# Finer row steps per expert, and slots of their own for the weights of the last four experts

## The reference

```
logits = x @ gate_w.T                       # 2048 tokens, 64 experts
topk_w, topk_ids = top_k(softmax(logits), 6)
topk_w = topk_w / (sum(topk_w) + EPS)
g, u = split(x @ w_gate_up[e].T)            # 256 -> 2 x 176, for the chosen experts
routed = sum over chosen e of (silu(g) * u * topk_w[e]) @ w_down[e].T
out = routed + shared
```

## Time and profile before

| | us |
|---|---|
| median of the runs (797.34, 799.22, 3540.21) | 799.22 |
| the profiled execution | 796.76 |
| its span | 795.0 |
| start of the expert stage's first transposes on PE | 475.6 |
| end of the last add of the 64 experts | 767.6 |

### The profile page before, as it was taken

One profiled execution on the slowest core, in us unless ns is written; L12 is line 12 of the kernel. 1 busy time (PEld: TensorE's weight loads), 2 busy tenths in 40 slices (PEclk: granted clock), 3 DMA queues, 4 the chain that ended last, 5 costly groups with the idle time before them and its releaser, 6 DMA issues.

```text
span 795.0 us, 12309 instructions
## 1 busy us (share of the span) xinstructions
PE 634.9 (80%) x3072; PEld 481.3 (61%) x3072; DVE 473.9 (60%) x1598; ACT 285.2 (36%) x641; POOL 432.6 (54%) x482
## 2 busy tenths in 40 slices
PE   3688984864998957989888639999999889899930
PEld 2344541532887736767666528888888767677720
DVE  4887785998587777777776333445444434444422
ACT  2146666773244422434334303233323223222200
POOL 2477877220244422566666652576666666577750
PEclk9799998797899977999999769999999999999975
DMA  6347555585288854555563377999999999999667
GB/s 225 123 136 249 202 171 179 180 278 221 75 311 289 318 162 160 188 194 188 193 219 111 101 233 220 248 250 230 241 259 225 231 235 215 215 220 241 98 142 268
DMA packets 86518, 163.88 MB, mean 206 GB/s; under 512 B 11200, under 2 KB 51584, under 8 KB 86464
## 3 DMA queue, kind: packets, MB, share of 16 engines
q1 hardware_dynamic: 64736, 134.26, 51.2%
q0 software_dynamic: 20864, 28.08, 19.2%
q10 hardware_dynamic: 864, 0.93, 0.3%
HBM read 91.51 MB, written 71.71 MB: 205 GB/s over the span
## 4 chain that ended last, share of the span: by engine, by line
PE 34%; DMA 20%; DVE 18%; issue 14%; POOL 8%; another core or an unknown queue 3%; ACT 1%; DVEq 1%; SPq 0%; POOLq 0%; ACTq 0%
DMA acc<-hh,toki 18%; PE psum L839 5%; PE psum L915 5%; PE psum L1072 5%; POOL xs_rows L738 3%; PE psum L994 3%; DVE hh L1620 2%; PE psum L1076 2%; PE psum L1085 2%; POOL acc L778 2%; PE psum L811 2%; PE psum L906 2%; PE psum L821 2%; PE psum L1060 1%
## 5 line engine op out<-in xcount | busy, mean ns | idle before, releaser
L778 POOL DMA_INDIRECT acc<-hh,toki x128 | 188.1, 1469 | 103.8 <-DMA acc<-hh,toki 51.7
L1918 DVE TENSOR_SCALAR hh<-psum,wtok 96x256 f32<-96x256 f32 (+2 forms) x128 | 55.9, 477 | 152.0 <-PE psum L1090 78.9
L738 POOL DMA_INDIRECT xs_rows<-Z,slot x96 | 96.4, 1004 | 58.4 <-DVE slot L1796 32.4
L1072 PE MATMUL psum<-qT,Z 128*128 128x192 f32 (+2 forms) x512 | 106.1, 351 | 0.0
L1072 PEld LDWEIGHTS psum<-qT,Z 128*128 128x128 f32 x512 | 87.6, 192 | 3.0 <-issue 0.4
L656 POOL TENSOR_TENSOR rstd<-mv,neghalf 128x1 f32<-128x1 f32 (+1 forms) x48 | 36.6, 763 | 77.3 <-DVE mv L1408 77.3
L1345 ACT ACTIVATE qT<-psum 128x384 f32<-128x384 f32 (+2 forms) x64 | 33.9, 530 | 113.3 <-PE psum L1060 96.4
L1085 PE MATMUL psum<-Z,hh 128*96 128x256 f32 (+2 forms) x256 | 61.9, 385 | 14.1 <-issue 8.9
L839 PE MATMUL psum<-wt,hTs 128*128 128x512 f32 x128 | 60.6, 617 | 9.4 <-ACT hTs L1169 9.4
L994 PE MATMUL psum<-qT,wt 128*128 128x256 f32 (+1 forms) x192 | 52.6, 431 | 9.7 <-DVE H L1801 8.9
L1085 PEld LDWEIGHTS psum<-Z,hh 128*96 128x96 f32 (+2 forms) x256 | 42.9, 173 | 28.4 <-issue 12.6
(11 more groups left out here) (337 smaller groups left out, 1233.8 us busy)
## 6 DMA issues: line engine op xcount, KB each, us to landing
Z<-in_wexp SPq DMA_DIRECT2D x66, 496.0 KB
xs_rows<-fill SPq DMA_DIRECT2D x64, 272.0 KB, 3.2
kv_rows<-Z SPq DMA_DIRECT2D x12, 688.0 KB, 3.8
Z<-xs_rows SPq DMA_DIRECT2D x32, 204.0 KB
kvb<-kv_rows SPq DMA_DIRECT2D x8, 688.0 KB
Z<-co_rows SPq DMA_DIRECT2D x8, 688.0 KB
Z<-kv_rows SPq DMA_DIRECT2D x8, 688.0 KB
Z<-xs_rows SPq DMA_DIRECT2D x16, 272.0 KB
```

What stands on the lines that cost most here:

```text
L738: pool.indirect_dma_start(out=xs_rows[:, :], out_offset=bass.IndirectOffsetOnAxis(ap=slot[:, t, k:k + 1], axis=0), in_=H[:, t, :], in_offs ...
L778: pool.indirect_dma_start(out=acc[s % 2][:, :], out_offset=bass.IndirectOffsetOnAxis(ap=toki[0:p, g, j:j + 1], axis=0), in_=y_sb[0:p, s, j ...
L1072: m = pe.matmul(pA[par][:, g * CAP:g * CAP + 2 * p], wgu_sb[:, s, k, g * P:(g + 1) * P], xT[:, par, k, 0:2 * p], start=(k == 0), stop=(k = ...
L1918: m = dve.tensor_scalar(y_sb[0:p, s, j, :], pY[par][0:p, j * D:(j + 1) * D], wtok[0:p, g, j:j + 1], None, ALU.mult)
```

## The change

Rows: `PARTS` goes from (128, 128, 112, 112, 96, 96, 96, 96) to (128, 120, 112, 104, 96, 96, 88, 80), so that iterations 1, 3, 6 and 7 have fewer rows, and every iteration from 1 on has a phase of its own. The capacity of each rank is worked out on DVE from six steps of 16 instead of two of 32.

Weights: those of the last four ranks go to four slots of their own, in `X` and in a free part of `hidden`, and are loaded right behind those of ranks 4 to 7, after a wait for `seeded` (all rows of the stream are written) and `ov_ready` 2 (the overflow tables are done). The last refill then leaves out its last four weight loads. PE reads these slots for the last four ranks. The two semaphores of each quarter of the accumulators at the end become one.

```diff
-    PARTS = (128, 128, 112, 112, 96, 96, 96, 96)
-    STEPS = ((16, 32.0), (32, 32.0))
-    PHASES = ((1, 2), (2, 3), (3, 4), (4, 5), (5, 8))
+    PARTS = (128, 120, 112, 104, 96, 96, 88, 80)
+    LESS = (8, 16, 24, 32, 48, 56)
+    PHASES = ((1, 2), (2, 3), (3, 4), (4, 5), (5, 6), (6, 7), (7, 8))
...
+        lastw = X[:, :, :].rearrange("p t d -> p (t d)")[:, 0:4 * (2 * GU + D)].rearrange("p (a f) -> p a f", a=4)
+        lastd1 = hidf[:, 1536:2048].rearrange("p (a d) -> p a d", a=2)
...
+            sp.wait_ge(seeded, 16 * 2 * NT)
+            sp.wait_ge(ov_ready, 2)
+            for s in range(4):
+                who = expert_at(E - 4 + s)
+                sp.dma_start(lastw[:, s, :], wexp[who]).then_inc(last_in, 16)
+                at = ODD * (s % 2)
+                sp.dma_start(lastd1[at:at + F1, s // 2, :], wd1[who]).then_inc(last_in, 16)
...
-            def refill(i, near, far):
+            def refill(i, near, far, groups):
                 for g in range(0, WS, 2):
                     for j in range(2):
                         next_rows(WS * i + 6 + g + j, (g + 2 + j) % 4, near if g < 2 else far)
-                    for j in range(2):
+                    for j in range(2 if g < groups else 0):
...
-            for lo_, hi_ in ((0, 1), (1, 2), (2, 3), (3, 4), (4, 7)):
+            for lo_, hi_ in ((0, 1), (1, 2), (2, 3), (3, 4), (4, 5), (5, 6), (6, 7)):
                 with sp.Fori(lo_, hi_) as i:
-                    refill(i, PARTS[lo_], PARTS[lo_ + 1])
+                    refill(i, PARTS[lo_], PARTS[lo_ + 1], WS if hi_ < E // WS - 1 else WS - 4)
...
-            def up(i, s, p, first):
+            def up(i, s, p, first, last=False):
                 e, par = WS * i + s, s % 2
-                pe.wait_ge(w_in[s], 32 * i + 32)
+                if last:
+                    pe.wait_ge(last_in, 128)
+                else:
+                    pe.wait_ge(w_in[s], 32 * i + 32)
+                w, s = (lastgu, s - 4) if last else (wgu_sb, s)
...
-            link(dve.tensor_scalar(cap_e[:, 0:1], rank_e[:, 0:1], float(STEPS[0][0]), STEPS[0][1], ALU.is_ge, ALU.mult))
-            link(dve.tensor_scalar(cap_e[:, 1:2], rank_e[:, 0:1], float(STEPS[1][0]), STEPS[1][1], ALU.is_ge, ALU.mult))
-            link(dve.tensor_tensor(cap_e[:, 0:1], cap_e[:, 0:1], cap_e[:, 1:2], ALU.add))
+            link(dve.tensor_scalar(cap_e[:, 0:1], rank_e[:, 0:1], float(LESS[0]), 16.0, ALU.is_ge, ALU.mult))
+            for r in LESS[1:]:
+                link(dve.tensor_scalar(cap_e[:, 1:2], rank_e[:, 0:1], float(r), 16.0, ALU.is_ge, ALU.mult))
+                link(dve.tensor_tensor(cap_e[:, 0:1], cap_e[:, 0:1], cap_e[:, 1:2], ALU.add))
...
-                dve.wait_ge(early_in[c], 16)
-                dve.wait_ge(back_in[c], 16)
+                dve.wait_ge(back_in[c], 32)
```

More of the change, by code:

```diff
@@ L169, in build @@
         hidf = hidden[:, :, :].rearrange("p a n -> p (a n)")
+        lastw = X[:, :, :].rearrange("p t d -> p (t d)")[:, 0:4 * (2 * GU + D)].rearrange("p (a f) -> p a f", a=4)
+        lastgu = lastw[:, :, 0:2 * GU].rearrange("p a (k f) -> p a k f", k=2)
+        lastd0 = lastw[:, :, 2 * GU:2 * GU + D]
+        lastd1 = hidf[:, 1536:2048].rearrange("p (a d) -> p a d", a=2)
         hid0 = hidf[:, 0:512].rearrange("p (a t) -> p a t", a=2)
@@ L360, in build @@
         sum_done = sem("sum_done")
-        early_in = [sem(f"early_in{c}") for c in range(4)]
+        last_in = sem("last_in")
         back_in = [sem(f"back_in{c}") for c in range(4)]
@@ L603, in _ @@
             for c in range(4):
-                sp.dma_start(back[1][:, 4 * c:4 * c + 4, :], acc_lines[1][:, 4 * c:4 * c + 4, :]).then_inc(early_in[c], 16)
+                sp.dma_start(back[1][:, 4 * c:4 * c + 4, :], acc_lines[1][:, 4 * c:4 * c + 4, :]).then_inc(back_in[c], 16)
             sp.wait_ge(o_yr, 2 * n + 1)
@@ L1071, in up @@
                     for k in range(2):
-                        m = pe.matmul(pA[par][:, g * CAP:g * CAP + 2 * p], wgu_sb[:, s, k, g * P:(g + 1) * P],
+                        m = pe.matmul(pA[par][:, g * CAP:g * CAP + 2 * p], w[:, s, k, g * P:(g + 1) * P],
                                       xT[:, par, k, 0:2 * p], start=(k == 0), stop=(k == 1))
@@ L1075, in up, with down_pair @@
                 for k in range(2):
-                    m = pe.matmul(pC[par][0:GU - 2 * P, 0:2 * p], wgu_sb[:, s, k, 2 * P:GU],
+                    m = pe.matmul(pC[par][0:GU - 2 * P, 0:2 * p], w[:, s, k, 2 * P:GU],
                                   xT[:, par, k, 0:2 * p], start=(k == 0), stop=(k == 1))
                 m.then_inc(guC_done, 1)
-            def down_pair(i, s, p):
+            def down_pair(i, s, p, last=False):
                 pe.wait_ge(xhid_ready, WS * i + s + 2)
@@ L1085, in down_pair @@
                         pe.matmul(pY[q][0:p, j * D:(j + 1) * D], hid0[:, q, j * p:(j + 1) * p],
-                                  wd0_sb[:, s + q, :], start=(j == 0), stop=False, skip_group_check=True)
+                                  lastd0[:, s - 4 + q, :] if last else wd0_sb[:, s + q, :], start=(j == 0), stop=False, skip_group_check=True)
                 for j in range(2):
@@ L1090, in down_pair, with pair @@
                         m = pe.matmul(pY[q][0:p, j * D:(j + 1) * D], hid1[r, q, j * p:(j + 1) * p],
-                                      wd1_sb[r, s + q, :], start=False, stop=True, skip_group_check=True)
+                                      lastd1[r, (s - 4) // 2, :] if last else wd1_sb[r, s + q, :],
+                                      start=False, stop=True, skip_group_check=True)
                         if j == 1:
                             m.then_inc(y_done, 1)
-            def pair(i, g, p, before):
+            def pair(i, g, p, before, end=False):
                 h, a, o = i - (g == 0), (g - 2) % WS, p if g else before
                 transposes(i, g, p, False)
-                up(h, a + 1, o, False)
+                up(h, a + 1, o, False, end and g == 6)
                 transposes(i, g + 1, p, False)
-                up(i, g, p, False)
-                down_pair(h, a, o)
+                up(i, g, p, False, end and g >= 4)
+                down_pair(h, a, o, end and g == 6)
             pe.wait_ge(base_ready, NPAIR)
@@ L1117, in _ @@
                     for g in range(0, WS, 2):
-                        pair(i, g, PARTS[lo_], PARTS[lo_ - 1])
-            up(E // WS - 1, WS - 1, PARTS[-1], False)
-            down_pair(E // WS - 1, WS - 2, PARTS[-1])
+                        pair(i, g, PARTS[lo_], PARTS[lo_ - 1], hi_ == E // WS)
+            up(E // WS - 1, WS - 1, PARTS[-1], False, True)
+            down_pair(E // WS - 1, WS - 2, PARTS[-1], True)
             n = pe.value_load(nov_i[0:1, 0:1], min_val=1, max_val=MAXB // 2)
```

## The result

| | before | after |
|---|---|---|
| median of four runs each, on one chip, us | 798.28 (794.72 to 3540.21) | 804.39 (801.5 to 807.34) |
| profiled execution / its span, us | 796.76 / 795.0 | 803.07 / 801.3 |

The ratio is 1.0088, with an interval at 95% of 1.0048 to 1.0129. It leaves out the run of 3540.21 us; without it the median before is 797.34. But the interval excludes 1: the change costs about 7 us, where the forecast had about none.

What follows compares the result with a forecast made beforehand. The landing of adds among weight and row transfers was taken to bound most of the expert stage. 796.76 + 0.8 + 4.2 - 0.4 - 0.3 - 0.3 - 3.5 = 797.3, plus 1.5 for undisturbed runs, gave 799 us; range 793.5 to 805.

Steps and rivals of the forecast that it cites:

- What bounds it: Expert stage: PE sets the pace up to rank 16, then the landing of adds among weight and row transfers.
- Chain, +0.8: Capacity chain on DVE: eight more linked instructions delay PE's table by 1.4 us, 0.6 hidden, so 0.8 us reaches the stage.
- Early loads, +4.2: Start of the expert stage: four early weight loads on SP delay rank 4's rows, stalling PE 4.2 us; clock loss taken as 0.
- Rival 3: Start of the stage: early loads cost the whole 6.9 us and the clock's 1.8, +4.5, 803 us; chance 0.10.
- Fewer rows, -0.4, -0.3, -0.3: Iterations 1, 3 and 6 at 120, 104 and 88 partitions: the adds' pace quickens, saving 0.4, 0.3 and 0.3 us.
- Rival 1: Row numbers not multiples of 16 spread badly over DMA engines; iterations 1, 3, 6 pace 9.08 us, 802 us; chance 0.22.
- Tail, -3.5: Last iteration from rank 51: without late loads adds step at 1.73 us, saving 3.0; 80 partitions save 0.5 more.
- Rival 4: Tail: the late loads were hidden, POOL's steps after rank 51 stay, the -3.5 is missing, 802 us; chance 0.08.

Runs made afterwards that it cites:

- l112: The kernel before with 112 instead of 96 partitions in its last four iterations; 800.57 us, 1.0071 of before.
- e5_chain: The kernel before with its two capacity steps of 32 written as six of at most 16, same sums; 796.85 us, 1.0014 of before.
- e3_behind: The whole change with the four early weight loads moved behind the row loads of ranks 4 and 5 on SP's queue; 795.69 us, 1.0006 of before.
- e2_weights: The kernel before with only the change's weight slots, early loads and shorter last refill, rows as before; 800.62 us, 1.0070 of before.
- e4_sixteens: e3_behind with partitions (128, 128, 112, 112, 96, 96, 96, 80), and three capacity steps instead of six; 792.81 us, 0.9979 of before.
- l104: The kernel before with 104 instead of 96 partitions in its last four iterations; 807.0 us, 1.0133 of before.
- l104_loads: l104 with the row loads rounded up to 112 partitions, the adds staying at 104; 805.08 us, 1.0113 of before.
- e1_rows: The kernel before with only the change's row numbers and capacity chain, all weights loaded late as before; 797.49 us, 1.0026 of before.
- e7_rounded: e3_behind with row loads, weighing and adds rounded up to multiples of 16 partitions, PE and ACT keeping the finer steps; 794.71 us, 0.9991 of before.
- e6_back: e4_sixteens with SP's load of the second accumulator waiting until the first overflow add has landed; 793.48 us, 0.9989 of before.
- e8_both: e7_rounded with SP's load of the second accumulator waiting until the first overflow add has landed; 793.93 us, 0.9986 of before.

## Why the forecast was wrong

Two steps of the sum failed. The early loads' term left out the granted clock behind a wait that was found rightly. And the terms for fewer rows and for the tail took an add's time from a straight line through 128, 112 and 96 partitions, which 120, 104 and 88 are not on. One by one:

**What bounds it: right for most of the stage, and not used to its end.** The adds hold the pace behind rank 16. Then what an add costs on POOL is a price of its own, and the part of the change that touches it was the one to bound from above too. l112 also shows how little rows are worth there: with 112 partitions for 96 from rank 32 on, ranks 32 to 48 took 69.37 us, before 69.81; the clear loss came behind rank 48. (These are single traces: e5_chain, with before's rows, took 67.13.)

**Chain, +0.8: right in DVE's rows, not told from nothing in the time.** The table that PE waits for was done at 459.69 for 457.39:

```profile
456.08 0.13 DVE L1865 TENSOR_SCALAR ranks_e<-ranks_e 64x1 f32<-64x1 f32 x1
459.44 0.25 DVE L1874 CAST nb_b<-nb_j 64x128 bf16<-64x128 int32 x1
```

2.3 later, of which 0.9 was there when the chain began (456.08 for 455.21). The 3.3 us by which the stage started late after is more than the chain can give, and e3_behind, with the same chain, started at 476.72: 1.1 late. The start scatters from trace to trace: with the chain of six steps it lies at 474.2 (e5_chain) to 478.9 (after), 476.7 on average in six traces, with two or three steps at 473.4 to 476.4, 475.1 on average in eight. So the rest is taken for scatter; nothing tested it.

**Early loads, +4.2: the right place, mis-sized.** The issue order and the 6.7 us on SP came as worked out. That the wait did so too (3.75, forecast 3.9) is luck in part: from issue to use rank 4's rows took 499.19 - 494.69 = 4.50 us, where the forecast had 2.9 from the first rows, and PE came to them 1.84 late, which hid that. In e2_weights PE was on time but for 0.2, and the wait was 4.90. What failed is "I take 0 since this pause is about half as long" for the clock. A pause of 3.75 us was enough: the granted clock went to the lower level, 1.7 us in the first eight products after, 2.5 in all in e2_weights. Wait and clock are 5.5 after and 7.4 in e2_weights; moving the loads gave 6.5. So 2.3 us are missing from this term. Rival 3 had the clock's share in it (1.8), but its wait of 6.9 us did not come.

**Fewer rows, -0.4, -0.3, -0.3: the sign failed for 104, and the price of an add for all three.** The durations were carried on as a line through 128, 112 and 96. Between them it isn't one: 120, 104 and 88 cost more than 128. For 104 the runs have the price against 112: 6.4 us in 32 experts, so an estimate of 1.6 for the eight of iteration 3, where the forecast had -0.3. For 120 and 88 only the durations and e3_behind beside e4_sixteens speak. Rival 1 had the right numbers under suspicion and the wrong transfer. Row loads do spread over fewer engines, by their packets. The Trainium skill's rule (DMA: Bandwidth & Descriptors, Why a DMA increments its semaphore by 16 and not by 1) gives 15, 13 and 11 engines, so 1 + 3 + 5 end packets less for each of 8 loads. That is 72, and 320 row packets less make 392, which is what q1 fell by:

```profile
q1 hardware_dynamic: 64736, 134.26, 51.2%
```

```profile
q1 hardware_dynamic: 64344, 133.57, 51.0%
```

l104 against l112 agrees: 65248 - 64896 = 352, 8 row packets and 3 end packets less for each of 32 loads. But l104_loads shows that this spread costs nothing measurable; the adds' filling-up does. Its price in POOL's time is 16 x (0.05 + 0.12 + 0.15) = 5.1 us against 128, 112 and 96, about the 5.5 by which the group rose. Not all of it reaches the end, since POOL waits for landings anyway: e1_rows lost 2.1 us with the chain's 1.1 in it. The pace after is 8.90 a pair at 120 (35.61 us for four pairs, rank 8 to 16), 8.94 at 104 (35.77) and 8.24 at 88 (32.94), where rival 1 had 9.08 in all three. The first two say little: ranks 16 to 24, with 112 partitions in all of these kernels, took 9.18 a pair before, 8.71 after and 8.45 in e3_behind. The third stayed at before's 8.23 though the four late loads are gone from it; with 96 partitions and the same weights it was 7.89 in e2_weights and 7.91 in e4_sixteens.

**Tail, -3.5: it needs adds of 96 partitions in iteration 6, and more.** From rank 51's first add to the last it took 46.18 us, before 46.21; the forecast asked for 42.75. Behind rank 51 POOL did stop waiting for landings, but up to rank 56 each step was 1.57 + 0.30 = 1.87 us, not 1.73: 18.80 us from 728.95 to 747.75, where e4_sixteens took 17.31 and the forecast had 17.1. That is half of the 3.4 missing. The other 1.7 lie behind rank 56 (27.38 us for 15 steps, 25.65 by the forecast). There POOL stood idle ahead of ranks 61, 62 and 63, though their results were ready: DVE had weighed ranks 62 and 63 by 765.58. After, the first adds of ranks 61 and 62, and DVE's weighing of 62 and 63:

```profile
765.37 1.42 POOL L790 DMA_INDIRECT acc<-hh,toki  x1 [0.62 <-issue]
769.77 1.41 POOL L790 DMA_INDIRECT acc<-hh,toki  x1 [1.27 <-issue]
763.60 0.87 DVE L1936 TENSOR_SCALAR hh<-psum,wtok 80x256 f32<-80x256 f32 x2 [3.12 <-issue]
764.71 0.87 DVE L1936 TENSOR_SCALAR hh<-psum,wtok 80x256 f32<-80x256 f32 x2 [0.23 <-DMA acc<-hh,toki]
```

With the 0.50 before the last add that is 1.5 us more than the usual 0.30 each. e3_behind has 1.99 and 0.49 ahead of ranks 61 and 63, there with the landing of earlier adds as the releaser; e7_rounded has none. Which of its differences took these waits away was not tried, and their cause stays open. PE was slow earlier, but POOL had no wait over 0.31 us from 730 to 765, so these adds were not late by it:

```profile
730.47 2.47 PE L1101 MATMUL psum<-Z,hh 128*88 128x256 f32 x8 [2.02 <-DVE hh L1925]
735.40 2.42 PE L1088 MATMUL psum<-qT,Z 128*128 128x160 f32 x8
738.93 1.29 PE L1088 MATMUL psum<-qT,Z 128*128 128x160 f32 x8
```

After a wait of 2.02 us for DVE the clock was at the lower level, and the products for 80 partitions took 2.42 for 1.29. With the adds at 96 partitions in iteration 6 the gain is there in part or nearly in full: 44.90 us in e2_weights, 44.76 in e6_back, 44.11 in e4_sixteens, 43.19 in e8_both and 43.06 in e7_rounded. Rival 4, that the late loads were hidden, is wrong; its number came about by other causes.

**Sum.** By the runs: chain +1.1, early loads +6.5, and rows and tail together -0.6, which is e3_behind's +0.5 less the chain. (That these make up the 7.0 is no proof, since the loads' share is the change less e3_behind.) The forecast had -4.5 for rows and tail and 4.2 for the loads. Each rival was priced as if it came alone. The clock's share of rival 3, the odd row numbers of rival 1 and the missing tail of rival 4 came together, the last two by other mechanisms than theirs. That 804.39 lies inside the range owes something to its width.

**What the adds' delay of 9.0 became.** The time rose by 6.3 in the profiled execution. The end gave back 2.7, most of it between the two adds of the overflow. POOL's two overflow adds and SP's load between them, before and after:

```profile
768.90 1.56 POOL L794 DMA_INDIRECT acc<-hh,toki  x1 [1.32 <-DVE hh L1961]
777.63 1.55 POOL L794 DMA_INDIRECT acc<-hh,toki  x1 [7.18 <-DMA acc<-hh,toki]
769.54 1.97 SPq L604 DMA_DIRECT2D Z<-acc  x4
```

```profile
776.85 1.57 POOL L806 DMA_INDIRECT acc<-hh,toki  x1 [0.30 <-issue]
782.21 1.56 POOL L806 DMA_INDIRECT acc<-hh,toki  x1 [3.79 <-DMA acc<-hh,toki]
778.40 2.02 SPq L616 DMA_DIRECT2D Z<-acc  x4
```

5.36 us between the adds for 8.73, with SP's 2 MB 1.55 us behind the first add instead of 0.64. e6_back and e8_both kept the 2 MB back until the first add had landed: the second add came 4.53 and 4.64 us behind the first, and the time gained nothing. So the order goes with an earlier second add in these traces and is no lever.

## What to carry to other kernels

Where a queue is served in order, put prefetches that nobody needs for 200 us behind the loads that someone needs next: the same transfers cost 6.5 us in one place and nothing measurable two loads later. Before a size gets a finer step, look at every kind of transfer that uses it at the new values: a straight line through three sizes says nothing of those between, and here the finest step made the bounding instruction longer. A wait of a few us on TensorE can cost its clock as well, as it did here; add the slow products behind it to the wait.

## What the runs showed of the hardware

An indirect add of 104 partitions takes 1.60 us on POOL and, by the packet counts, is filled up to 128 with 24 near empty packets; at 112 it takes 1.47 and is not filled up. 120 and 88 partitions cost 1.60 and 1.57, both more than 128 at 1.55. The packet counts of row loads fit 15, 13 and 11 engines at 120, 104 and 88 partitions. At 104 that had no measurable cost (l104 beside l104_loads), with engines 0.91 to 0.98 busy from 620 to 740 us. And TensorE's granted clock fell to the lower level behind waits of 2.02, 3.75 and 4.90 us in these traces.
